# Second FFN: how many blocks' scatters wait for landings while the mixer runs

## The chip, the cores and the metric

One Trainium2 chip, one core of it, one launch. The metric is the device time of one execution in microseconds (us), the median of the runs. Engines are named as in the profile: PE (TensorE), DVE (VectorE), ACT (ScalarE), POOL (GpSimd), SP (SyncE, which here issues plain DMAs).

## The reference

Three layers on x of 4 sequences x 1,024 tokens x 128 features (4,096 tokens). The first and the third are the same mixture-of-experts FFN with the same weights:

```python
x = x + 0.5 * ffn(layernorm(x))        # 8 experts, top 2, and a shared one
x = x + attn(layernorm(x))             # mixer: conv, a recurrence over time, gated FFN
x = x + 0.5 * ffn(layernorm(x))

# ffn:
shared = (silu(x @ sw1) * (x @ sw2)) @ sw3
probs = softmax(x @ rw + rb); w, idx = top_k(probs, 2); w = w / sum(w)
gates = sum(w[..., None] * one_hot(idx, 8))
h = silu(x @ ew1[e]) * (x @ ew2[e]);  eout = h @ ew3[e]     # every expert e
out = shared + sum(eout * gates)
```

The middle layer keeps a state per head through a scan over the 1,024 tokens of each sequence; its own gated FFN has 352 hidden features.

## The kernel before

The 4,096 tokens are 8 blocks (NB) of 512, each 4 tiles (TT) of 128 rows. Blocks of the first FFN are turns 0 to 7, those of the second are turns 8 to 15. Both FFNs sort the rows by expert: each block is normalised (`dve_stats`, `pool_rstd`, `dve_norm` into `rows`), its logits and its rows' places are found (`dve_route`, `dve_places`, which ends with `pos_ready`), and POOL writes each row to two places of the DRAM tensor `xs`, with 8 indirect DMAs of 128 rows a block (`pool_scatter`, L710). All raise the semaphore `scattered` by 16 when they have landed. Then the shared expert is added, SP reads the 72 sorted tiles back from `xs` once `scattered` is at 1,024 per FFN and the last shared up-projection is done (L453 and the wait behind it), and the experts run over them; POOL scatters their answers to `ys` (L726), which SP reads back for the sum.

The second FFN's front is spread into the mixer. The mixer is a software pipeline: `in_order` calls one `body` per engine for steps n = -8 to 16, and `do(work, at(-k))` runs `work` for block n - k, if there is one. On POOL `route_rstd` is done for block n - 7 and `route_scatter` for block n - 9, in four pairs of scatters, of which the first stands ahead of `route_rstd`, the second behind it, the others behind `h_add`. `early` lets only blocks 0 to 4 (EARLY = 5) through; those of blocks 5 to 7 are issued behind the mixer by `pool_ffn(1)`, 24 in a row. So step 12 holds the scatters of block 3 and the rstd of block 5, step 13 the scatters of block 4 and the rstd of block 6, step 14 only the rstd of block 7, the last of all.

Each engine takes its instructions in program order; a wait on a semaphore holds what is behind it on that engine. Before each pair in the mixer POOL waits until every scatter before it has landed (L707 to L709). On DVE the norm of block 6 (turn 14, L1404) stands ahead of the mixer's last addition to x (L1324), and behind that come the statistics of block 7. The second FFN begins on PE (`pe_ffn_again`) when that last addition is done (`mixer_done`); the norm of block 7 stands behind the first two shared products on DVE (L1488), and the route of block 5 behind it; PE waits for what this route has chosen (`chosen`, L1989) ahead of the second block's second product.

Of the kernel before, what the change touches and what calls it, by code (L numbers as in the profile page):

```python
# [16 lines left out]
NB = TOK // BT  # L17
# [10 lines left out]
GROUP = 16  # L28

EARLY = 5  # L30
BACK = (4, NB)
LN_EPS = 1e-5

# [55 lines left out]
def macaron(nc, A, out):  # L89
    ctx = ExitStack()  # L90
    with ctx:
# [295 lines left out]
        def early(block):  # L387
            return block if block and SQ * block[0] + block[1] < EARLY else None

# [20 lines left out]
        def _(sp):  # L410
# [33 lines left out]
            for call in range(2):  # L444
# [18 lines left out]
                for r in range(YRING):  # L463
                    sp.wait_ge(y_stored[r], 32 * (NPAIR // YRING) * (call + 1))
                ring = BACK[call]
                for n in range(NB):
# [42 lines left out]
        def pool_mixer(pool, ffn_own):  # L509
# [134 lines left out]
            def route_scatter(b, q, k):  # L644

                pool_scatter(pool, NB + SQ * b + q, (2 * k, 2 * k + 1))
# [55 lines left out]
        def pool_scatter(pool, turn, which=range(2 * TT)):  # L702

            n = turn % NB
            pool.wait_ge(pos_ready, turn + 1)
            for i in which:
                if NB <= turn < NB + EARLY and i % 2 == 0:  # L707

                    pool.wait_ge(scattered, 16 * (turn * 2 * TT + i))  # L709
                pool.indirect_dma_start(xs, bass.IndirectOffsetOnAxis(pos[:, n, i:i + 1], 0),  # L710
                                        rows[:, n * TT + i % TT, :], None).then_inc(scattered, 16)
# [18 lines left out]
        def pool_ffn(pool, own, call):  # L730
            if call == 0:
                pool_rstd(pool, own, 0)
                pool_route_const(pool)
                pool_rstd(pool, own, 1)
                for n in range(NB):
                    pool_scatter(pool, n)
                    if n == 0:
                        pool_rstd(pool, own, 2, 2)
                    if n == 1:
                        pool_rstd(pool, own, 4, 4)  # L740
                pool_clear_features(pool)
                pool_mixer_const(pool)
            else:

                for n in range(EARLY, NB):
                    pool_scatter(pool, NB + n)
            for p in range(NPAIR):
                pool_answers(pool, call, p)
# [238 lines left out]
        def act_route_xt(act, n, answers):  # L987
            act.wait_ge(rx_ps_ready, n + 1)
            if n:

                act.wait_ge(logits_ps_ready, NB + n)
            act.activation(xr[:, :], answers, ACT.Copy).then_inc(rx_ready, 1)
# [8 lines left out]
        def act_silu(act, turn, k):  # L1001
            step = 2 * turn + k
            act.wait_ge(a_ps_ready, step + 1)
            if step >= 2:
                act.wait_ge(hid_done, step - 1)
            act.activation(silu_a[:, k, :], ps_a[:, k, :], ACT.Silu).then_inc(silu_done, 1)  # L1006
# [56 lines left out]
        def act_ffn_again(act):  # L1063
            act_xt(act, NB)
            act_xt(act, NB + 1)
            for n in range(NB):

                act_silu(act, NB + n, 0)
                if EARLY + n < NB:
                    act_route_xt(act, EARLY + n, ps_t)  # L1070
                act_silu(act, NB + n, 1)
# [365 lines left out]
        def dve_places(dve, own, turn, answers=ps_k):  # L1437

            n = turn % NB
            dve.wait_ge(rank_ps_ready, turn + 1)  # L1440
            own.step(dve.tensor_tensor(place[:, :].rearrange("p (t e) -> p t e", t=TT),
                                       answers[:, 0:TT * NE].rearrange("p (t e) -> p t e", t=TT),
                                       base[:, n:n + 1, :].broadcast_to([P, TT, NE]), ALU.add))
            dve.tensor_tensor(base[:, n + 1, :], base[:, n, :], answers[:, TT * NE:TT * NE + NE], ALU.add).then_inc(rank_read, 1)
            own.settle()
            own.step(dve.tensor_tensor(placed[:, :, :].rearrange("p (k t) e -> p k (t e)", k=2), hot[:, turn % 2, :, :],
                                       place[:, :].rearrange("p (a c) -> p a c", a=1).broadcast_to([P, 2, TT * NE]), ALU.mult))
            own.settle()
            own.step(dve.reduce_sum(pos_f[:, :], placed[:, :, :], axis=mybir.AxisListType.X))
            own.settle()  # L1450
            dve.tensor_copy(pos[:, n, :], pos_f[:, :]).then_inc(pos_ready, 1)
# [30 lines left out]
        def dve_hid(dve, turn, k):  # L1482
            step = 2 * turn + k
            dve.wait_ge(silu_done, step + 1)
            dve.wait_ge(b_ps_ready, step + 1)
            if turn >= 2:
                dve.wait_ge(down_ps_ready, turn - 1)
            dve.tensor_tensor(hid[:, turn % 2, k, :], silu_a[:, k, :], ps_b[:, k, :], ALU.mult).then_inc(hid_done, 1)  # L1488
# [44 lines left out]
        def dve_combine(dve, own, call, n):  # L1533

            dve.wait_ge(block_in[n], 16 * (call + 2))
            for k in range(2):
                for t in range(TT):
                    at = n * TT + t
                    r = dve.scalar_tensor_tensor(x[:, at, :], y_in[call][:, n % BACK[call], t, k * P:(k + 1) * P], share[:, k, at:at + 1],
                                                 x[:, at, :], ALU.mult, ALU.add)  # L1540
# [63 lines left out]
        def dve_ffn_again(dve, own):  # L1604
            dve.wait_ge(mixer_done, NB)
            for n in range(NB + 1):

                if n < NB:
                    dve_hid(dve, NB + n, 0)
                if 1 <= n <= NB - EARLY:  # L1610
                    dve_places(dve, own, NB + EARLY + n - 1)
# [596 lines left out]
```

## Time and profile before

| | |
|---|---|
| three runs | 786.61, 892.56 and 2213.87 us |
| median | 892.56 us |
| span of the profiled execution, first to last instruction | 783.3 us |
| its run time, taken as the shortest shown | 786.61 us, 3.3 us around the span |
| PE / DVE / ACT / POOL busy | 644.3 / 547.1 / 424.9 / 520.4 us |
| L710, scatters to xs | 128, 127.2 us busy, 993 ns each |
| L726, scatters to ys | 144, 141.0 us busy, 980 ns each |

"Busy" is the time in which an engine executes; POOL's row for a scatter is the time in which it makes and issues the transfer, not the transfer. Two parts of the profile say what that costs: the chain that ended last, which goes back from the last instruction to whatever released each one, and the timelines of the engines, where idle time ahead of an instruction stands in brackets with what ended it.

### The profile page before, as it was taken

How to read it: one execution, taken by the hardware profiler on the slowest of the kernel's cores; microseconds unless marked ns; L12 is line 12 of the kernel's file. 1: busy time of each engine (PE TensorE's matmuls, PEld its weight loads, DVE VectorE, ACT ScalarE, POOL GpSimd, SP SyncE). 2: the span in 40 equal slices, each digit the busy share in tenths (PEclk: the TensorE clock that was granted, in tenths of full speed). 3: DMA queues.
4: the chain of work that ended last, by engine and by line, in shares of the span. 5: the costliest groups of instructions: out<-in, count | busy, mean ns of one | idle time of the engine just before them, and what ended most of it. 6: DMA issues, size and time to landing. Idle time of an engine off the chain costs nothing.

```text
span 783.3 us, 13708 instructions
## 1 busy us (share of the span) xinstructions
PE 644.3 (82%) x3768; PEld 475.4 (61%) x3768; DVE 547.1 (70%) x1706; ACT 424.9 (54%) x745; POOL 520.4 (66%) x656
## 2 busy tenths in 40 slices
PE   3478979999916288989999998999968999999950
PEld 2245558888812045656575756577635667888840
DVE  4666756666539659897989999999743645666637
ACT  1122225455406999998999998764212324545525
POOL 3787775666645676896978869686765713666660
PEclk9989989999966678999999999999988999999995
DMA  9411223333242000000000000000000212333219
GB/s 266 159 46 52 82 67 80 93 89 85 65 142 84 0 1 1 0 2 1 1 2 1 2 15 15 14 15 15 28 27 28 69 45 76 87 89 91 81 30 318
DMA packets 49368, 46.34 MB, mean 59 GB/s; under 512 B 8456, under 2 KB 42861, under 8 KB 49296
## 3 DMA queue, kind: packets, MB, share of 16 engines
q1 hardware_dynamic: 40592, 28.54, 13.0%
q0 software_dynamic: 8704, 16.93, 6.7%
q8 instruction: 34, 0.56, 0.3%
q14 instruction: 38, 0.31, 0.1%
HBM read 25.30 MB, written 21.19 MB: 59 GB/s over the span
## 4 chain that ended last, share of the span: by engine, by line
PE 35%; POOL 24%; issue 15%; DVE 13%; ACT 8%; DMA 4%; POOLq 1%; SPq 0%; DVEq 0%; ACTq 0%
POOL ys L726 11%; POOL xs L710 10%; PE ps_tr L1662 4%; PE ps_go L1662 3%; DMA xs<-rows,pos 2%; PE ps_tr L2064 2%; PE ps_go L2012 2%; PE ps_go L2051 1%; PE ps_go L1833 1%; PE ps_tr L1850 1%; PE ps_go L1837 1%; POOL rstd L700 1%; PE ps_b L1884 1%; PE ps_a L2002 1%; PE ps_go L1883 1%
## 5 line engine op out<-in xcount | busy, mean ns | idle before, releaser
L726 POOL DMA_INDIRECT ys<-arena,dest x144 | 141.0, 980 | 99.8 <-issue 65.4
L710 POOL DMA_INDIRECT xs<-rows,pos x128 | 127.2, 993 | 58.8 <-issue 35.8
L1006 ACT ACTIVATE silu_a<-ps_a 128x512 f32<-128x512 f32 x32 | 19.1, 597 | 62.1 <-PE ps_a L2002 62.1
L2064 PE MATMUL ps_tr<-w_down_e,arena 128*128 x384 | 50.7, 275 | 0.0
L1521 DVE TENSOR_TENSOR hid<-silu_a,ps_a 128x512 f32<-128x512 f32 x36 | 24.8, 688 | 34.1 <-ACT silu_a L1026 34.1
L1521 DVE TENSOR_TENSOR hid<-silu_a,ps_b 128x512 f32<-128x512 f32 x36 | 24.8, 688 | 34.1 <-ACT silu_a L1026 34.1
L2064 PEld LDWEIGHTS ps_tr<-w_down_e,arena 128*128 128x128 f32 x384 | 46.7, 192 | 0.0
L1035 ACT ACTIVATE arena<-ps_go 128x512 f32<-128x512 f32 x72 | 42.6, 592 | 2.0 <-PE ps_go L2051 2.0
L1488 DVE TENSOR_TENSOR hid<-silu_a,ps_b 128x512 f32<-128x512 f32 x32 | 21.9, 686 | 31.0 <-PE ps_b L2004 29.1
L2051 PE MATMUL ps_go<-ident,hid 128*128 128x128 f32 x288 | 43.2, 273 | 0.2
L1026 ACT ACTIVATE silu_a<-ps_a 128x512 f32<-128x512 f32 x36 | 21.5, 597 | 38.1 <-PE ps_a L2040 38.1
L1026 ACT ACTIVATE silu_a<-ps_b 128x512 f32<-128x512 f32 x36 | 21.5, 597 | 37.7 <-PE ps_b L2040 37.7
L2051 PEld LDWEIGHTS ps_go<-ident,hid 128*128 128x128 f32 x288 | 35.5, 140 | 10.1 <-DVE hid L1521 0.8
L1018 ACT ACTIVATE xt_hi<-ps_tr 128x256 fp32r<-128x256 f32 x48 | 18.5, 385 | 35.0 <-PE ps_tr L2025 35.0
L1833 PE MATMUL ps_go<-arena,state 128*128 128x128 f32 x128 | 31.3, 329 | 7.4 <-DVE us L1291 6.5
L2012 PEld LDWEIGHTS ps_go<-w_shared_down,hid 128*128 128x128 f32 x256 | 31.6, 197 | 7.6 <-issue 7.6
L1963 PE MATMUL ps_tr<-ident,rows 128*128 128x128 f32 x64 | 13.5, 349 | 25.7 <-DVE rows L1404 19.9
L2012 PE MATMUL ps_go<-w_shared_down,hid 128*128 128x128 f32 x256 | 32.1, 280 | 1.7 <-DVE x L1493 1.7
L1833 PEld LDWEIGHTS ps_go<-arena,state 128*128 128x128 f32 x128 | 21.5, 201 | 19.4 <-issue 13.9
L2038 PE MATMUL ps_a<-up_hi,xt_hi 128*128 x72 | 31.8, 442 | 0.9 <-DVE xt_lo L1506 0.8
L1662 PE MATMUL ps_go<-arena,w_tap 128*128 128x512 f32 x64 | 32.2, 649 | 0.0
L2038 PE MATMUL ps_b<-up_hi,xt_hi 128*128 x72 | 31.6, 439 | 0.0
(368 smaller groups left out, 2032.5 us busy)
## 6 DMA issues: line engine op xcount, KB each, us to landing
arena<-xs SPq DMA_DIRECT2D x144, 65.0 KB, 1.9
rows<-ys SPq DMA_DIRECT2D x8, 512.0 KB, 3.7
arena<-ys SPq DMA_DIRECT2D x8, 512.0 KB, 6.8
ys<-arena,dest POOLq DMA_INDIRECT x144
x<-in_L_attn_x SPq DMA_DIRECT2D x8, 256.0 KB, 4.4
arena<-in_L_ffn_ew SPq DMA_DIRECT2D x4, 512.0 KB, 6.9
xs<-rows,pos POOLq DMA_INDIRECT x128
out<-x SPq DMA_DIRECT2D x8, 256.0 KB, 4.7
```

Source lines behind the costliest of these rows:

```text
L710: pool.indirect_dma_start(xs, bass.IndirectOffsetOnAxis(pos[:, n, i:i + 1], 0), rows[:, n * TT + i % TT, :], None).then_inc(scattered, 16)
L726: pool.indirect_dma_start(ys, bass.IndirectOffsetOnAxis(dest[:, i:i + 1], 0), y_out[:, p % YRING, j, :], None, bounds_check=2 * TOK - 1, o ...
L1026: act.activation(silu_a[:, p % 2, :].rearrange("p (j h) -> p j h", j=2), ps_pair[p % 2][:, :, 0:HID], ACT.Silu).then_inc(silu_e_done, 1)
L1035: act.activation(hid_t[:, p % 2, :], ps_d, ACT.Copy).then_inc(ht_ready, 1)
L1488: dve.tensor_tensor(hid[:, turn % 2, k, :], silu_a[:, k, :], ps_b[:, k, :], ALU.mult).then_inc(hid_done, 1)
L1521: dve.tensor_tensor(hid[:, p % 2, 0, :].rearrange("p (j h) -> p j h", j=2), silu_a[:, p % 2, :].rearrange("p (j h) -> p j h", j=2), ps_pai ...
L1662: r = pe.matmul(target, weights(k), zt[:, shift:shift + BT], start=(k == 0), stop=(k == taps - 1))
L1833: pe.matmul(pb["o"][:, at], state[:, k % 2, p * P:(p + 1) * P], cfs[:, q, k * P:(k + 1) * P], start=True, stop=False)
L2012: r = pe.matmul(ps_d[:, t * P:(t + 1) * P], hid[:, turn % 2, k, t * P:(t + 1) * P], w_shared_down[:, k, :], start=(k == 0), stop=(k == 1))
L2038: pe.matmul(target, xt_hi[:, p % 2, mine], hi, start=True, stop=False)
L2051: r = pe.transpose(ps_d[:, at:at + P], hid[:, p % 2, 0, at:at + P], ident[:, :])
L2064: r = pe.matmul(ps_answers(p)[:, j * P:(j + 1) * P], hid_t[:, p % 2, at:at + P], w_down_e[:, bass.ds(which[2 * p + j], 1), k, :].rearrange ...
```

## The change

One constant is added, and it takes the place of EARLY in the condition of the wait. EARLY, and so the place of every scatter, stays. The waits ahead of the pairs of turns 11 and 12 (blocks 3 and 4, 16 scatters, 8 waits) are gone; those of blocks 0 to 2 (12 waits) stay. No instruction is added, taken away or moved on any engine.

```diff
 EARLY = 5
+PACED = 3
 BACK = (4, NB)
 LN_EPS = 1e-5
...
             n = turn % NB
             pool.wait_ge(pos_ready, turn + 1)
             for i in which:
-                if NB <= turn < NB + EARLY and i % 2 == 0:
+                if NB <= turn < NB + PACED and i % 2 == 0:
 
                     pool.wait_ge(scattered, 16 * (turn * 2 * TT + i))
                 pool.indirect_dma_start(xs, bass.IndirectOffsetOnAxis(pos[:, n, i:i + 1], 0),
```

## Rows read from the trace of the kernel before

**Rows 1.** The page, part 4: the chain that ended last, by engine and line.
```profile
PE 35%; POOL 24%; issue 15%; DVE 13%; ACT 8%; DMA 4%; POOLq 1%; SPq 0%; DVEq 0%; ACTq 0%
POOL ys L726 11%; POOL xs L710 10%; PE ps_tr L1662 4%; PE ps_go L1662 3%; DMA xs<-rows,pos 2%; PE ps_tr L2064 2%; PE ps_go L2012 2%; PE ps_go L2051 1%; PE ps_go L1833 1%; PE ps_tr L1850 1%; PE ps_go L1837 1%; POOL rstd L700 1%; PE ps_b L1884 1%; PE ps_a L2002 1%; PE ps_go L1883 1%
```

**Rows 2.** Waits of POOL: who waited for what, us in total, times, longest us.
```profile
POOL xs L710 <- DMA xs<-rows,pos: 10.9, 5, 2.4
```

**Rows 3.** The chain in time, 545 to 650 us: start, length, what.
```profile
585.15 2.29 DMA xs<-rows,pos
...
595.17 1.05 POOL rstd L700
...
596.32 1.12 DVE rows L1404 x4
```

**Rows 4.** Timeline of POOL: start, length, instruction, [idle before <-releaser].
```profile
463.44 1.10 POOL L710 DMA_INDIRECT xs<-rows,pos  x1 [0.19 <-issue]
...
558.80 1.01 POOL L710 DMA_INDIRECT xs<-rows,pos  x1
...
563.17 1.10 POOL L710 DMA_INDIRECT xs<-rows,pos  x1 [0.68 <-issue]
...
575.11 0.96 POOL L710 DMA_INDIRECT xs<-rows,pos  x1 [2.10 <-DMA xs<-rows,pos]
...
579.43 0.96 POOL L710 DMA_INDIRECT xs<-rows,pos  x1 [2.09 <-DMA xs<-rows,pos]
...
582.03 1.04 POOL L700 TENSOR_TENSOR rstd<-var_eps,minus_half 128x4 f32<-128x4 f32 x1
583.76 1.09 POOL L710 DMA_INDIRECT xs<-rows,pos  x1 [0.68 <-issue]
...
588.21 0.96 POOL L710 DMA_INDIRECT xs<-rows,pos  x1 [2.09 <-DMA xs<-rows,pos]
...
592.58 0.96 POOL L710 DMA_INDIRECT xs<-rows,pos  x1 [2.15 <-DMA xs<-rows,pos]
...
602.50 0.96 POOL L710 DMA_INDIRECT xs<-rows,pos  x1 [0.30 <-issue]
...
630.33 0.96 POOL L710 DMA_INDIRECT xs<-rows,pos  x1 [0.30 <-issue]
```

**Rows 5.** L710 from 0 to 105 us: duration in ns, min/median/max.
```profile
L710 POOL DMA_INDIRECT xs<-rows,pos x64: 955/962/1307, 17.4 to 103.8; - x64
```

**Rows 6.** L710 from 430 to 600 us, the same columns.
```profile
L710 POOL DMA_INDIRECT xs<-rows,pos x40: 957/962/1447, 454.8 to 593.8; - x40
```

**Rows 7.** Timeline of DVE.
```profile
583.18 1.12 DVE L1404 TENSOR_SCALAR rows<-x,mv,rstd 128x128 f32<-128x128 f32 x4 [6.20 <-POOL rstd L700]
584.21 0.68 DVE L1324 TENSOR_TENSOR x<-x,ps_tr 128x512 f32<-128x512 f32 x1
...
585.84 0.38 DVE L1392 BATCH_NORM_AGGREGATE mv<-stats 128x2 f32<-128x6 f32 x4
...
592.90 0.69 DVE L1488 TENSOR_TENSOR hid<-silu_a,ps_b 128x512 f32<-128x512 f32 x1 [1.36 <-PE ps_b L2004]
```

**Rows 8.** Timeline of PE.
```profile
577.03 2.94 PE L1897 MATMUL ps_tr<-w_down,arena 128*128 128x128 f32 x24 [0.78 <-DVE arena L1318]
584.95 1.11 PE L1963 MATMUL ps_tr<-ident,rows 128*128 128x128 f32 x4 [4.97 <-DVE x L1324]
...
599.53 0.18 PE L1989 MATMUL ps_go<-chosen,earlier 128*128 128x32 bf16 x1 [3.28 <-DVE chosen L1434]
...
641.34 1.02 PE L2004 MATMUL ps_b<-arena,w_shared 128*128 128x512 f32 x2
```

**Rows 9.** Stretches: busy us of each engine, then PEclk (granted clock).
```profile
566.00:580.00 14.00, 12.21 (x72) 8.24 (x72) 7.57 (x39) 2.48 (x4) 8.92 (x11) 1.00 0.07 24
...
585.00:590.00 5.00, 4.22 (x11) 2.58 (x12) 1.18 (x8) 1.52 (x3) 2.45 (x3) 0.52 0.12 40
...
599.50:603.00 3.50, 3.47 (x13) 1.55 (x14) 1.25 (x6) 0.60 (x1) 1.59 (x2) 0.58 0.06 19
```

## The prediction

> **What bounds the kernel now.** I read first the chain that ended last. No engine holds it alone: PE has 35% of it, POOL 24%, and POOL's two kinds of scatter have 11% and 10% [rows 1]; the landings of scatters to xs are in it with 2%, some 16 us of 783.3. So a wait for a landing can be on the path. The waits of POOL say how much is plainly such: 10.9 us in five waits [rows 2]. The chain in order of time then shows where. At 585.15 us it goes through a landing of 2.29 us; it leaves POOL with the rstd of block 7 at 595.17 and goes on with DVE's norm of that block at 596.32 [rows 3]. The reader is to see that the end of the mixer hangs on POOL, and that POOL is slowed there by its own waits.
>
> POOL's timeline gives each wait its place [rows 4]. Of the five, the longest belongs to block 2 and stays. The other four lie in blocks 3 and 4: 2.10 at 575.11, 2.09 at 579.43, 2.09 at 588.21, 2.15 at 592.58. The first scatter behind each of the two rstds is late as well: 0.68 us of idle at 563.17 and at 583.76, against 0.19 behind an earlier one at 463.44, where the wait had long been met. The profile calls these "issue", but both come a landing's time behind the previous scatter.
>
> **What the change removes, step by step.** Of its eight waits two cost nothing now. The first of block 3 starts at 558.80 with no idle time ahead of it [rows 4]. The third pair of block 3 has POOL's h_norm and h_add between it and the pair before, which take longer than a landing. The cover stays, since nothing is moved; were it gone, each would cost the 1.8 us of its neighbours. The six others leave a gap of 0.30 us, as ahead of the unwaited scatter at 602.50 [rows 4], or of 0.19 behind an rstd:
>
> - 563.17: 0.68 - 0.19 = 0.49
> - 575.11: 2.10 - 0.30 = 1.80
> - 579.43: 2.09 - 0.30 = 1.79
> - 583.76: 0.68 - 0.19 = 0.49
> - 588.21: 2.09 - 0.30 = 1.79
> - 592.58: 2.15 - 0.30 = 1.85
>
> Sum 8.2 us for the rstd of block 7, and the first three, 4.1 us, for the rstd of block 6 (582.03, ends 583.07 [rows 4]).
>
> **Who takes it up.** DVE had waited 6.20 us for the rstd of block 6, with the mixer's last addition queued behind the norm (583.18, then 584.21); the statistics of block 7 end at 586.22, and PE had been idle 4.97 us for that addition [rows 7, 8]. PE's last mixer product, from 577.03, ends at 579.97 [rows 8], 0.5 sooner with POOL's first gain, and the addition would move to 580.1, so it is still DVE's queue that is late and all of the 4.1 us passes: the second FFN starts on PE at 580.9. The rstd of block 7 needs the statistics, now at 582.1, and POOL comes to it at about 587.0, so they don't hold it.
>
> Next, the norm of block 7 on DVE. It needs the rstd, which would end at 596.2 - 8.2 = 588.0, and DVE's second shared product, which ends at 593.59 - 4.1 = 589.5 [rows 7]. **What is late next** is thus that product: the norm moves from 596.32 to 589.6, by 6.8 us, and by the full 8.2 only if PE brings the product 1.4 us sooner.
>
> It may, by its clock. From 585 to 590 us the granted clock was 0.52, the lower level of 1.2 GHz, after the 4.97 us of idle; in 566 to 580, with pauses of about 1 us, it was 1.00, or 2.4 GHz [rows 8, 9]. The pause shrinks from 4.97 to about 1.4 us (579.5 to 580.9). If the clock stays up, 4.22 us of busy PE become 2.0 shorter at most (4.22 x 0.48), less what ACT's copies between them cover. Bounds 0 and 2.0 us, of which 1.4 count.
>
> The second pause, 3.28 us ahead of 599.53 for what the route of block 5 chose, shrinks to about 0.6 us (PE would be through at 596.2 - 4.1 = 592.1, the choice comes at 592.7), or to 1.2 in the other case. Behind it 3.5 us ran at 0.58 [rows 8, 9]; at 1.00 they take 1.5 us less. Bounds 0 and 1.5; I take 1.5, since pauses of that length left the clock at 1.00 in 566 to 580.
>
> The sum: 6.8 at least, 6.8 + 1.5 = 8.3 with the second clock term, 8.2 + 1.5 = 9.7 with both. Between the last two I take the middle, **9.0 us**.
>
> **What lies behind.** The 24 unwaited scatters of blocks 5 to 7 follow the route of block 5 and move with it; the last, at 630.33, is 11 us ahead of PE's last shared product at 641.34 [rows 4, 8], which also holds SP's reads of xs. So they bind neither before nor after. From there the experts' part has no tie to an earlier time: it shifts whole.
>
> **A page against it.** Scatters beside busy DVE took 957 to 1447 ns, median 962, and in the first FFN, with no waits, 955 to 1307 [rows 5, 6]. The Trainium skill, SBUF — State Buffer, in its section on SBUF's two separate sides, says that VectorE in a two-port mode locks GpSimd out of writing descriptors, so that a transfer issued by POOL can stand still for the length of a DVE instruction. By that rule the sum is the one of rival 1, not 9.0. This trace bears out little of it: the median is 5 ns off the minimum.
>
> **The time.** 783.3 - 9.0 = 774.3 us of span, with 3.3 us around it **777.6 us**. That stands on the shortest run shown, 786.61, to which the profiled execution belongs. The median, 892.56, is 106 us above, and the third run 1427 above; no row explains either. A like change on the level of the median would give 883.
>
> **The rivals.**
>
> 1. *Half of it is eaten* (0.12): unwaited scatters take longer beside DVE. If each of the 12 that follow 563 us took 0.49 us more, the worst seen over the median (1447 - 962), 5.8 of the 9.0 us would go: 783 us. It also stands for the norm of block 7 being held by something that I took to be covered. For: the 1447. Against: DVE is idle for much of 566 to 596, and 24 scatters in a row keep to 1.27 us.
> 2. *The excess of the longer runs sits in the waits* (0.15). If landings are what is slow there, 106 us over 20 waits is 5.3 each, and eight fewer give 42 more: 892.56 - 9 - 42 = 841. For: the only thing in this kernel that leaves the core unasked is DMA. Against: nothing shown of those runs.
> 3. *Slower* (0.13): with slow landings, unwaited scatters pile up, and each further one stalls in POOL's issue. In the longer runs the 88 + 144 unwaited transfers would carry the excess, 0.46 us each in the run of 892.56 and 6.2 in that of 2213.87; sixteen more add 7 or 98 us. It decides from (9.0 + 15.7) / 16 = 1.5 us per scatter on; below that it only eats the gain. A measured time in the 900s or above would be it. Against: in the profiled execution 88 run unwaited at 1.27 us apart.
> 4. *Nothing happens* (0.05): the waits were met by something else, such as the bare issue of POOL; then 786.6. The gaps of 0.30 beside those of 2.1 speak against it.
>
> The forecast itself has 0.55: of this some 0.12 is that the step holds and yet the number measured lies on the upper level, 875 to 895.
>
> **Range and chances.** The forecast's own range is 772 to 785: gain 6.8 to 9.7, and some us for how far the shortest run may lie from 786.6. With rivals 1, 2 and 4, and the upper level, the range goes from 770 to 895; rival 3 and the rest stay out. A difference of 2%, about 16 us, is what a measurement of this kernel can tell from no change. The forecast, 1.1%, is below it, and so are rivals 1 and 4: 0.60 for within 2%. Faster by more: rival 2, and the forecast if the two kernels' medians fall on different levels, 0.26. Slower by more: rival 3 and the same in reverse, 0.14.
>
> **What would show it.** In the profile after: no idle over 0.7 us ahead of any scatter from 558 us to the rstd of block 7, which starts near 587.0 and not 595.17; DVE's last addition near 580.1 and not 584.21; PE's pauses about 1.4 and 1 us in place of 4.97 and 3.28, with the granted clock near 1.00 behind both; and the rest as before, 9 us sooner. It is wrong if scatters there last over 1 us in the median, if the addition stays near 584 (another wait on DVE), or if the clock stays low behind the shorter pauses (then 6.8 us and 779.8).

## The result, and the profile after

| | before | after |
|---|---|---|
| runs | 785.39, 786.61, 892.56, 2213.87 us | 775.26, 777.01, 777.22, 778.66 us |
| median | 839.59 us | 777.12 us |
| profiled execution | span 783.3 | 775.26 us, span 773.5 |

Ratio 0.9893, 95% interval [0.9864, 0.9921]: 1.07% faster, 8.4 us of 786, and clear of no change. The ratio leaves out 892.56 and 2213.87, which have no like among the runs of the change. The profiled execution of the change is the fastest of its four (the spans of the others are 775.3, 775.5 and 776.9 us), so its trace shows somewhat more gain than the times do.

One figure ahead of the prediction is to be set right. The span of 783.3 us was taken to belong to the run of 786.61, with 3.3 us around it. In every later run the time is 1.7 to 2.2 us above the span, so it belongs to a run of about 785.3; the fourth run, 785.39, fits.

The page of the changed kernel, part 4, the chain that ended last:

```profile
PE 46%; POOL 18%; DVE 13%; issue 10%; ACT 8%; DMA 3%; SPq 1%; POOLq 0%; DVEq 0%; ACTq 0%
POOL xs L711 10%; POOL ys L727 5%; PE ps_tr L2065 4%; PE ps_tr L1663 4%; PE ps_go L2052 3%; PE ps_go L1663 3%; PE ps_go L2065 2%; PE ps_go L1834 2%; PE ps_a L2039 2%; PE ps_go L1838 2%; PE ps_a L2041 2%; PE ps_a L2040 2%; PE ps_go L2013 2%; PE ps_b L2041 2%; PE ps_b L2040 2%
```

POOL's share went from 24 to 18% and PE's from 35 to 46 [rows 1]. This doesn't measure the gain: the scatters to xs have 10% as before, and what fell, from 11 to 5%, is the share of the scatters to ys, which the change doesn't touch. The waits and the times do. POOL's waits for landings (us in total, times, longest us):

```profile
POOL xs L711 <- DMA xs<-rows,pos: 2.6, 1, 2.6
```

Five waits of 10.9 us have become one of 2.6, the one in block 2 that the change keeps [rows 2]. POOL's timeline (start us, length, instruction, idle before), then the durations of L711 (the old L710) from 555 to 600 us in ns, and the time from the issue of these scatters to their landing in us:

```profile
558.55 1.01 POOL L711 DMA_INDIRECT xs<-rows,pos  x1
...
562.44 1.10 POOL L711 DMA_INDIRECT xs<-rows,pos  x1 [0.20 <-issue]
...
572.41 0.95 POOL L711 DMA_INDIRECT xs<-rows,pos  x1 [0.30 <-issue]
...
574.93 0.96 POOL L711 DMA_INDIRECT xs<-rows,pos  x1 [0.30 <-issue]
...
577.54 1.04 POOL L701 TENSOR_TENSOR rstd<-var_eps,minus_half 128x4 f32<-128x4 f32 x1
578.78 1.09 POOL L711 DMA_INDIRECT xs<-rows,pos  x1 [0.20 <-issue]
...
581.44 0.96 POOL L711 DMA_INDIRECT xs<-rows,pos  x1 [0.30 <-issue]
...
583.96 0.95 POOL L711 DMA_INDIRECT xs<-rows,pos  x1 [0.30 <-issue]
...
586.55 1.04 POOL L701 TENSOR_TENSOR rstd<-var_eps,minus_half 128x4 f32<-128x4 f32 x1
...
621.67 0.95 POOL L711 DMA_INDIRECT xs<-rows,pos  x1 [0.30 <-issue]
```

```profile
L711 POOL DMA_INDIRECT xs<-rows,pos x23: 955/959/1098, 554.7 to 598.9; - x23
...
DMA to landing us min/median/max: 2.3/2.3/2.4
```

The six gaps of [rows 4] are now 0.20, 0.30, 0.30, 0.20, 0.30 and 0.30 us, and unwaited scatters take no longer: median 959 ns against 962 [rows 6], and none of them lands later than 2.4 us after its issue. The rstd of block 6 starts at 577.54 (was 582.03), that of block 7 at 586.55 (was 595.17). DVE's timeline:

```profile
578.69 1.21 DVE L1405 TENSOR_SCALAR rows<-x,mv,rstd 128x128 f32<-128x128 f32 x4 [2.21 <-POOL rstd L701]
579.73 0.68 DVE L1325 TENSOR_TENSOR x<-x,ps_tr 128x512 f32<-128x512 f32 x1
...
581.34 0.38 DVE L1393 BATCH_NORM_AGGREGATE mv<-stats 128x2 f32<-128x6 f32 x4
...
586.49 0.69 DVE L1489 TENSOR_TENSOR hid<-silu_a,ps_b 128x512 f32<-128x512 f32 x1 [1.36 <-PE ps_b L2005]
587.69 1.12 DVE L1405 TENSOR_SCALAR rows<-x,mv,rstd 128x128 f32<-128x128 f32 x4 [0.52 <-POOL rstd L701]
```

The last addition moved from 584.21 to 579.73, the norm of block 7 from 596.32 to 587.69 [rows 3, 7]. The norm still waits for the rstd (0.52 us), not for the shared product ahead of it, which ended at 587.18. PE's timeline, and the stretches (length, busy us of PE, PEld, DVE, ACT, POOL, then the granted clock):

```profile
576.53 2.94 PE L1898 MATMUL ps_tr<-w_down,arena 128*128 128x128 f32 x24 [0.78 <-DVE arena L1319]
580.46 0.66 PE L1964 MATMUL ps_tr<-ident,rows 128*128 128x128 f32 x4 [0.98 <-DVE x L1325]
...
590.91 0.18 PE L1990 MATMUL ps_go<-chosen,earlier 128*128 128x32 bf16 x1 [1.08 <-DVE chosen L1435]
...
631.43 1.02 PE L2005 MATMUL ps_b<-arena,w_shared 128*128 128x512 f32 x2
```

```profile
585.00:590.00 5.00, 4.83 (x24) 2.87 (x22) 3.06 (x20) 2.23 (x5) 2.25 (x3) 1.00 0.08 28
590.00:596.00 6.00, 5.09 (x40) 4.17 (x41) 2.75 (x12) 1.66 (x3) 2.90 (x3) 1.00 0.08 25
```

The pauses of 4.97 and 3.28 us have shrunk to 0.98 and 1.08, and the granted clock, 0.52 and 0.58 behind them before, is 1.00 throughout [rows 8, 9]. The last shared product ends 9.9 us sooner, the last scatter (621.67) is still 10 us ahead of it, and the span is 9.8 us shorter. To see what the clock's part is, take the way from PE's L1989 (599.53 before, 590.91 after) to the first scatter of an answer, which stands in POOL's timelines, of before and of after:

```profile
657.26 0.99 POOL L726 DMA_INDIRECT ys<-arena,dest  x1 [25.98 <-DVE arena L1531]
```

```profile
647.34 1.00 POOL L727 DMA_INDIRECT ys<-arena,dest  x1 [24.71 <-DVE arena L1532]
```

57.73 us before, 56.43 after: 1.3 us less. With the 8.6 by which L1989 came sooner that is 9.9, all of the 9.8. That the 1.3 is the clock's is borne out by the traces further down, under "The clock alone".

### The profile page after: what moved, and what is told of

It reads as the page before. It is cut to its first block, busy times and chain, and to the rows that moved or that the text cites. A ratio compares the mean times of both kernels' runs of the same rounds, so it can differ in the third digit from the quotient of the medians.

```text
span 773.5 us, 13700 instructions
## 1 busy us (share of the span) xinstructions
PE 641.4 (83%) x3768; PEld 473.3 (61%) x3768; DVE 546.6 (71%) x1706; ACT 424.6 (55%) x745; POOL 519.9 (67%) x656
## 4 chain that ended last, share of the span: by engine, by line
PE 46%; POOL 18%; DVE 13%; issue 10%; ACT 8%; DMA 3%; SPq 1%; POOLq 0%; DVEq 0%; ACTq 0%
POOL xs L711 10%; POOL ys L727 5%; PE ps_tr L2065 4%; PE ps_tr L1663 4%; PE ps_go L2052 3%; PE ps_go L1663 3%; PE ps_go L2065 2%; PE ps_go L1834 2%; PE ps_a L2039 2%; PE ps_go L1838 2%; PE ps_a L2041 2%; PE ps_a L2040 2%; PE ps_go L2013 2%; PE ps_b L2041 2%; PE ps_b L2040 2%
## 5 line engine op out<-in xcount | busy, mean ns | idle before, releaser
L711 POOL DMA_INDIRECT xs<-rows,pos x128 | 127.2, 993 | 50.8 <-issue 36.0
L1838 PE MATMUL ps_go<-gram,tm 128*64 128x128 f32 x256 | 30.7, 321 | 0.0
```

What stands on the lines that cost most here:

```text
L1838: r = pe.matmul(pb["o"][i * DH:(i + 1) * DH, at], tm[:, k % 2, h * DH:(h + 1) * DH], gram[:, k % 2, :, h, :], start=False, stop=True)
```

## The experiments

Ratios are to runs of the kernel before on the same chip. The level differs between chips: on two the kernel before takes 785 us, on three others 850. Each was used in one session, so a chip and a session can't be told apart. A number is compared only within one chip.

**What a comparison can tell.** The constant at 5 makes a copy.

```diff
-PACED = 3
+PACED = 5
```

> The changed source with the constant at 5, so every wait is as before: a copy of the kernel before. It measures what the comparison itself can tell. Theory: ratio 1.000, interval within 0.4% either way, so a gain of 1.1% is well clear. Rival: the copies differ by 1% or more, and then the measured 1.1% could be chance. It also shows how often a run of the waits-everywhere kernel is far above 786 us; the theory has no opinion on that.

On a chip at 851 us: 0.9948 [0.9910, 0.9986]; the copy is off by 0.5%. Again:

> The copy of the kernel before, on a chip where it takes about 785 us. Theory: ratio 1.000 with an interval of 0.3% or less either way, so that 1.07% is clear of it. Rival: it is off by 0.5% as on the chip at 850 us, and half of the measured gain could be that.

It fell on a chip at 853 us: 1.0019 [0.9987, 1.0051]. So there 0.5% is not to be trusted and 1% is about the limit. The question for 785 us was not answered by a copy; the nearest thing is the variant with products in the pauses, further down, at 1.0005 [0.9981, 1.0028].

The copy also tells of the long level. POOL's waits for landings in it, and ACT's two largest waits:

```profile
POOL xs L711 <- DMA xs<-rows,pos: 12.9, 7, 2.6
```

```profile
ACT silu_a L1007 <- remote: 50.5, 7, 16.6
ACT xt_hi L1019 <- remote: 46.2, 18, 3.3
```

POOL's waits for landings are 12.9 us in 7 waits, against 10.9 in 5 at 785 us, so no more than 2 of the 65 us are theirs. ACT meanwhile waits nearly 100 us for something that the profile calls "remote" and doesn't know, on a kernel with one core. The chain that ended last has it too:

```profile
PE 41%; DVE 15%; issue 14%; another core or an unknown queue 10%; ACT 10%; POOL 6%; DMA 4%; SPq 0%; POOLq 0%; DVEq 0%; ACTq 0%
```

10% of 850.9 us is 85 us, as large as the excess. All ten traces from the chips at 850 us have such lines, and none of the ten at 785 has one. The scatters themselves are no slower: the median is 959 ns to xs and 981 to ys, against 962 and 982 before. What the unknown releaser is stays open.

**Block 4 alone.**

```diff
-PACED = 3
+PACED = 4
```

> Waits dropped for block 4 alone (4 waits, 79.43 us range after 579). Theory: the rstd of block 6 comes 1.8 us sooner, the rstd of block 7 5.9 us sooner; the norm of block 7 is then held by DVE's second shared product at 591.8 (4.5 us) or, if the clock stays up behind the first pause (about 3.2 us), by the rstd (5.9); 1.5 us more from the clock behind the second pause. Sum 6.0 to 7.4 us, ratio 0.991 to 0.992. Rival (only the sum of waits counts, no clock): 4.5 to 5.9.

At 851 us: 0.9879 [0.9830, 0.9929]. The repeat at 785 us:

> Block 4's waits dropped alone, once more, on a chip where the kernel before takes about 785 us. Theory as before (waits plus clock): 6.0 to 7.4 us. Rival (waits alone): 4.5 to 5.9.

0.9918 [0.9894, 0.9942], 6.4 us of 784.9. DVE's norm of block 7, and two stretches:

```profile
593.21 1.11 DVE L1405 TENSOR_SCALAR rows<-x,mv,rstd 128x128 f32<-128x128 f32 x4
```

```profile
585.00:590.00 5.00, 4.33 (x9) 2.19 (x10) 0.04 (x1) 1.72 (x3) 3.98 (x6) 0.50 0.16 53
...
599.50:603.00 3.50, 3.50 (x24) 2.70 (x23) 1.25 (x8) 1.05 (x2) 2.76 (x3) 1.00 0.18 57
```

The norm starts with no idle ahead of it: the shared product holds it, since the clock behind the first pause is still low (0.50). The second stretch is at 1.00. That is the case "held by the second shared product, clock back behind the second pause" of the expectation. Its size is not met in the trace: the norm came at 593.21 in place of 591.8, so 3.1 us sooner and not 4.5, and the span is 4.5 us shorter and not 6.0. The profiled run is the slowest of the six. The times, 6.4 us with an interval of 4.6 to 8.3, hold 6.0 and most of the rival's 4.5 to 5.9 as well; it is the trace that speaks for the clock.

**Block 3 alone.**

```diff
-                if NB <= turn < NB + EARLY and i % 2 == 0:
+                if NB <= turn < NB + EARLY and turn != NB + 3 and i % 2 == 0:
```

> Waits dropped for block 3 alone (4 waits). Theory: both rstds come 2.3 us sooner (0.49 + 1.80), the second pause of PE stays above 3 us and its clock low, so the run gains 2.3 us, ratio 0.997. Rival (the clock returns with either pause): 3.8 us. Rival (block 3's waits are covered): 0.

At 851 us: 0.9885 [0.9810, 0.9959], nearly as much as the whole change; with a copy off by 0.5% on that chip I don't read it. At 785 us:

> Block 3's waits dropped alone, once more, on such a chip. Theory: 2.3 us. Rival (clock comes back too): 3.8 or more; rival (covered): 0.

0.9974 [0.9957, 0.9991], 2.0 us. PE's timeline and two stretches behind:

```profile
597.45 0.18 PE L1989 MATMUL ps_go<-chosen,earlier 128*128 128x32 bf16 x1 [3.04 <-DVE chosen L1434]
```

```profile
599.50:603.00 3.50, 3.50 (x16) 2.98 (x15) 0.69 (x1) 0.14 (x1) 2.59 (x4) 0.50 0.12 38
603.00:605.50 2.50, 2.50 (x14) 2.50 (x13) 0.00 (x0) 0.46 (x1) 1.89 (x3) 0.50 0.17 53
```

The second pause is still 3.04 us and the clock behind it 0.50, as expected. The interval of the times, 0.7 to 3.4 us, leaves out both rivals (0 and 3.8). 2.0 and 6.4 add up to the 8.4 of the change, though with intervals this wide the exact fit is chance. The trace also shows what nobody expected: the clock came back only at about 605.6 us, 8 us behind the pause, where the kernel before had it back about 4 us behind a pause of 3.28. This profiled run, 785.5 us, is the slowest of twelve, and its span of 783.4 us shows none of the gain.

**No waits at all in the mixer.**

```diff
-PACED = 3
+PACED = 0
```

> No waits for landings in the mixer at all. Theory: blocks 0 to 2 have one wait that shows (2.44 us of idle at 553.17), and behind it POOL waits for DVE's us anyway (0.56 at 557.38), so at most 0.5 us beyond the measured change: ratio 0.988 to 0.990. Rival (waits in the middle of the mixer protect something): slower than the change, scatters over 1 us in the median, or some runs far above 780.

> No waits in the mixer, once more, on such a chip. Theory: no more than 0.5 us beyond the change, 774.5 to 777 us. Rival (the waits of blocks 0 to 2 protect something): slower than the change.

> No waits in the mixer, beside the changed kernel on one chip. Theory: within 0.5 us of the changed kernel. Rival: 1 to 2 us below it, if the wait of 2.44 us in block 2 was on the path.

0.9889 [0.9836, 0.9941] at 851 us, 0.9877 [0.9846, 0.9909] at 785, 0.9922 [0.9890, 0.9953] at 853, where the changed kernel itself, run beside it,

> The changed kernel again. Theory: 8.4 to 9.7 us, ratio 0.9877 to 0.9893. Rival: nearer to the sum of the waits' direct effect on the start alone (4.1 us, 0.995).

had 0.9914 [0.9882, 0.9945]. The waits of blocks 0 to 2 cost nothing that can be measured, nor do they protect anything that shows. The trace at 785 us (the slowest of its four runs) bears on the prediction in another way. PE's start, and a stretch behind it:

```profile
582.67 0.66 PE L1964 MATMUL ps_tr<-ident,rows 128*128 128x128 f32 x4 [1.39 <-DVE x L1325]
```

```profile
584.00:587.00 3.00, 2.90 (x7) 1.90 (x8) 0.00 (x0) 0.66 (x2) 2.39 (x3) 0.50 0.16 53
```

The pause is 1.39 us, just the length that was predicted for the change, and the clock behind it is 0.50. The shared product was late by it, and the norm of block 7 started behind that product, at 590.79.

**Which rstd counts.** All waits kept; the rstd of block 6 goes ahead of block 4's first pair. Two small helpers choose the block: but_last passes every block but 4, only_last passes 4 alone.

```diff
-                do(route_scatter, early(at(-9)), 0)
+                do(route_scatter, but_last(early(at(-9))), 0)
                 do(route_rstd, at(-7))
+                do(route_scatter, only_last(at(-9)), 0)
```

> All waits kept; in step 13 the rstd of block 6 stands ahead of block 4's first pair. Theory: that rstd ends near 578.7 in place of 583.07, so the second FFN starts on PE 4.2 us sooner, but the rstd of block 7 stays at 595.2 behind the same waits, and PE then waits longer in the second pause (about 8 us): gain 0 to 0.5 us. Rival (the start of the second FFN sets the end): 4.2 us, ratio 0.9947.

1.0060 [1.0035, 1.0086]: 4.7 us slower, which neither expected. POOL's timeline, PE's, and two stretches:

```profile
577.00 1.04 POOL L707 TENSOR_TENSOR rstd<-var_eps,minus_half 128x4 f32<-128x4 f32 x1
...
589.35 0.96 POOL L717 DMA_INDIRECT xs<-rows,pos  x1 [3.60 <-DMA xs<-rows,pos]
...
596.32 1.04 POOL L707 TENSOR_TENSOR rstd<-var_eps,minus_half 128x4 f32<-128x4 f32 x1
```

```profile
580.04 0.66 PE L1970 MATMUL ps_tr<-ident,rows 128*128 128x128 f32 x4 [0.78 <-DVE x L1331]
...
600.68 0.18 PE L1996 MATMUL ps_go<-chosen,earlier 128*128 128x32 bf16 x1 [11.26 <-DVE chosen L1441]
```

```profile
600.00:603.00 3.00, 2.32 (x11) 1.32 (x12) 1.84 (x9) 0.02 (x1) 0.73 (x1) 0.50 0.00 0
...
606.00:609.00 3.00, 3.00 (x15) 3.00 (x16) 0.00 (x0) 0.60 (x1) 2.20 (x3) 0.50 0.16 50
```

The start came at 580.04, nearly 5 us sooner, as expected. The rstd of block 7 didn't, and PE stood idle for 11.26 us. I had priced a longer pause at nothing. Behind it the clock was at the lower level until about 609 us, over 8 us; in the kernel before it is back after about 4. A landing was slow too (3.60 us of wait at 589.35), and the rstd starts at 596.32, 1.2 later than before. From L1996 to the first answer's scatter it is 60.60 us against 57.73. The 2.9 and the 1.2 are nearly all of the 4.2 us by which the span is longer. So the rstd of block 7 sets the end, and a start that runs ahead of it gains nothing. That it loses is shown by the times; that the longer pause is what held the clock down is not, since block 3 alone had 8 us at the lower level behind a pause of 3.04.

**The same waits elsewhere.** Block 4's last two pairs go behind the rstd of block 7.

```diff
                 do(route_rstd, at(-7))
+                do(route_scatter, only_last(at(-10)), 2)
+                do(route_scatter, only_last(at(-10)), 3)
...
-                do(route_scatter, early(at(-9)), 2)
+                do(route_scatter, but_last(early(at(-9))), 2)
...
-                do(route_scatter, early(at(-9)), 3)
+                do(route_scatter, but_last(early(at(-9))), 3)
```

> All waits kept; block 4's last two pairs stand behind the rstd of block 7 in place of ahead of it. Theory: that rstd comes as soon as its statistics, about 586.3 us, the norm is then held by DVE's second product (593.6, 2.7 us sooner), and the clock returns behind the shortened second pause (1.5 us): 4.2 us, ratio 0.9947, with the two pairs' waits moved to where PE covers them. Rival (what the waits cost is lost wherever they stand): 0.

0.9966 [0.9947, 0.9986], 2.7 us (1.1 to 4.2), with every wait still there. POOL's timeline and DVE's:

```profile
586.69 1.04 POOL L708 TENSOR_TENSOR rstd<-var_eps,minus_half 128x4 f32<-128x4 f32 x1
```

```profile
594.06 0.69 DVE L1496 TENSOR_TENSOR hid<-silu_a,ps_b 128x512 f32<-128x512 f32 x1 [1.77 <-PE ps_b L2012]
594.67 1.11 DVE L1412 TENSOR_SCALAR rows<-x,mv,rstd 128x128 f32<-128x128 f32 x4
```

The rstd comes at 586.69 as expected, and the norm is held by the shared product; but that came at 594.06 and not at 592.90, because the clock behind the first pause stayed low for longer this time: it is 0.50 from 590 to 592 us, and was 1.00 there before, though the pause is 5.04 us against 4.97. That is the missing 1.2 us. It is where the waits stand that makes them dear.

**The clock alone.** PE gets products that nobody reads, in both pauses; no wait of POOL is touched.

```diff
-            pe.wait_ge(mixer_done, NB)
             pe.wait_ge(rank_read, NB + EARLY)
+            for _ in range(5):
+                pe.matmul(ps_k[:, :], w_shared[:, 0:P], w_shared[:, 0:BT], start=True, stop=True)
+            pe.wait_ge(mixer_done, NB)
...
                     pe.wait_ge(rank_read, NB + late - 1)
+                    if n == 1:
+                        for _ in range(3):
+                            pe.matmul(ps_k[:, :], w_shared[:, 0:P], w_shared[:, 0:BT], start=True, stop=True)
                     pe_rank(pe, NB + late - 1)
```

> The kernel before with PE kept busy in its two pauses by products that nobody reads: five of 128x512 while it waits for the mixer's last addition, three before it waits for what block 5's route chose. No wait of POOL is changed. Theory: granted clock 1.00 from 585 to 603 us; the first pause gives nothing (the rstd of block 7 binds), the second 1.5 us: ratio 0.998. Rival (the clock has no part, only the waits): 0, or slower by the products. Rival (both stretches pay): 2.5 to 3.5 us.

1.0005 [0.9981, 1.0028]. PE's timeline and two stretches:

```profile
579.29 4.46 PE L2102 MATMUL ps_go<-w_shared 128*128 128x512 f32 x10
...
593.63 2.74 PE L2120 MATMUL ps_go<-w_shared 128*128 128x512 f32 x6
599.52 0.21 PE L1989 MATMUL ps_go<-chosen,earlier 128*128 128x32 bf16 x1 [3.15 <-DVE chosen L1434]
```

```profile
585.00:590.00 5.00, 4.22 (x17) 2.41 (x17) 1.33 (x7) 2.86 (x5) 2.55 (x3) 1.00 0.14 43
...
599.50:603.00 3.50, 3.48 (x12) 1.73 (x13) 1.32 (x6) 0.60 (x1) 1.52 (x2) 0.53 0.06 19
```

The first pause was filled and the clock behind it 1.00: no gain, since the rstd of block 7 binds. But PE came to the second pause sooner, the three products were done at 596.4, it stood idle for 3.15 us and fell to 0.53 again. So the second half of the test had failed. With six products there:

> As the kernel with products in PE's two pauses, but six in the second, so that it is busy until about 598.8 us. (With three, it stood idle for 3.15 us all the same and ran at the lower level behind that.) Theory: granted clock near 1.00 from 599.5 to 603 and a gain of 1.5 us, the waits untouched. Rival (the clock has no part in the gain): 0.

```profile
592.96 5.32 PE L2120 MATMUL ps_go<-w_shared 128*128 128x512 f32 x12
598.60 0.19 PE L1989 MATMUL ps_go<-chosen,earlier 128*128 128x32 bf16 x1 [0.33 <-DVE chosen L1434]
```

```profile
599.50:603.00 3.50, 3.50 (x25) 2.78 (x25) 1.09 (x4) 1.19 (x2) 2.13 (x3) 1.00 0.06 19
```

```profile
654.73 0.99 POOL L726 DMA_INDIRECT ys<-arena,dest  x1 [23.92 <-DVE arena L1531]
```

The pause is 0.33 us, the clock 1.00, and from L1989 to the first answer's scatter it is 56.13 us, 1.6 less than the 57.73 of before. The whole run gives 0.9993 [0.9975, 1.0012], 0.5 us, an interval from 2.0 us faster to 0.9 slower. The trace shows the term, the times don't resolve it.

The same way, in the nine traces at 785 us that keep the first FFN as it was, goes by the clock. Where it was 1.00 behind the second pause it takes 56.09 us (block 4 alone), 56.09 (no waits), 56.13 (this kernel), 56.25 (the waits moved) and 56.43 (the change). Where it fell it takes 57.73 (before), 57.77 (three products), 59.74 (block 3 alone) and 60.60 (the rstd of block 6 first).

**Waits everywhere.**

```diff
-                if NB <= turn < NB + EARLY and i % 2 == 0:
+                if turn + i > 0 and i % 2 == 0:
```

> A wait for landings ahead of every second scatter to xs, those of the first FFN and the last 24 of the second too (64 in all). Theory: each pair takes 4.3 us in place of 2.5; 32 pairs on the chain of the first FFN cost up to 57 us, the last 12 cost 22 less the 11 of slack, so 840 to 855 us. Rival for the long runs seen of the kernel before (they come with waits for landings): with three times the waits, most runs are far above the fastest. Without that tie the share of long runs is as before.

1.0736 [1.0699, 1.0773], 843.1 us median, within the 840 to 855 worked out; the five runs lie within 2 us of each other. The profile shows 92.3 us in 46 waits for landings, 81.4 more than before, of which 58 reached the time. They brought none of the five runs far above the others.

**The two together.** No waits, and both moves.

> No waits in the mixer; in step 13 the rstd of block 6 stands ahead of block 4's first pair, and block 4's last two pairs stand behind the rstd of block 7. Theory: PE's last mixer product (579.5) and DVE's second shared product bind now; the start gains 0.2 us and the norm of block 7 0.7, so 0.7 to 1.2 us below the changed kernel, ratio 0.987 to 0.988. Rival: the later scatters hold something, and it is as the changed kernel or slower.

> The reordered version without waits once more. Theory: 0.7 to 1.2 us below the changed kernel on a chip at 785 us. Rival: the same as the changed kernel.

> The changed kernel once more, beside e_best's kernel. Theory: ratio 0.988 to 0.990 on a chip at 785 us, 0.991 on one at 850.

At 853 us it had 0.9932 [0.9900, 0.9963], beside the changed kernel's 0.9914; at 850 us 0.9860 [0.9820, 0.9901], beside 0.9875 [0.9832, 0.9918]. Neither tells it from the changed kernel, and it never ran on a chip at 785 us.

## Why the prediction was right, and where it was not

- **The six gaps.** Predicted 8.2 us for the rstd of block 7, 4.1 for that of block 6. In the profile 8.62 and 4.49, of which the gaps are 8.2 and 4.1; 0.25 of each is older (558.55 against 558.80), 0.19 is a shorter L611 (1.04 us against 1.23). Shown.
- **Who takes it up.** The addition was predicted at 580.1, it came at 579.73. The norm of block 7 was to be held by the shared product at 589.6, or with the clock by the rstd at 588.1; it was the rstd, 587.69. With block 4 alone the product did hold it. Both branches have thus been seen.
- **The clock.** Predicted 1.00 behind pauses of about 1.4 and 1 us; so it was, behind 0.98 and 1.08. The term of 1.5 us measured 1.3 here and 1.6 in the variant with filled pauses. That the first pause left the clock up was in part luck: behind 1.39 us, in the kernel without waits, it fell to 0.50. What decides is not shown; the middle of the two branches, which the prediction took, says no more than that.
- **The sum.** 9.0 us predicted, 9.8 in the profiled execution (the fastest of four), 8.4 [6.2, 10.7] in the times; 777.6 against 777.12. That these last two are so close is luck in part: 3.3 us around the span was some 1.3 too much, and the 9.0 some 0.6 more than the times show. The times don't tell the branches of 8.3 and 9.7 apart.
- **The rival of DVE eating half** is out: the median of the unwaited scatters is 959 ns. The Trainium skill's rule on the shared port (SBUF — State Buffer, the section on its two separate sides) would have brought it about; in this stretch the longest scatter takes 1,098 ns on POOL, 0.14 us above the median, and the longest landing 2.4 us against a median of 2.3, so nothing here is held up for the length of a DVE instruction; in which mode DVE ran, no row shows. The single long one, 1,447 ns before, stands ahead of this stretch.
- **The step that failed is "range and chances".** "A difference of 2%, about 16 us, is what a measurement of this kernel can tell from no change": no row stood behind it, and it is not so. The change came out at 0.9893 [0.9864, 0.9921], and at 785 us the intervals of the other comparisons are 0.2 to 0.3% wide either way, so 1.1% is clear of no change. The measured difference does lie within 2%, and as a statement on its size the 0.60 held; as a forecast that nothing could be told, it was put on the wrong outcome. My own argument had only two cases with a gain well under 9 us, of 0.12 and 0.05. "Faster by about 1%, and told" was what the sum of the gaps said.
- **The base was left open too.** Against the median shown, 892.56, the forecast of 777.6 would be 13% faster; against the shortest run it is 1.1%. The sum was built on the shortest, and the runs bear that out: 1.07% against runs of 785 to 787 us. The level of 892.56 was never met again.
- **The upper end of 895** took in 892.56 as a level that the change could land on. The levels found are 785 and 850 us, and they go with the chip, as far as one session on each can tell: 50 runs of the kernel before lay between 782.8 and 791.2 on two chips, 59 between 842.8 and 860.6 on three. None came near 892.56 or 2213.87, and those two stay unexplained.
- **Rivals 2 and 3** tied the excess to landings or to unwaited scatters. With waits everywhere nothing strays in five runs, and with none in the mixer nothing does in 22; at 850 us POOL's waits for landings carry at most 2 of 65 us, and its scatters are as short as at 785. Both are out for the 850 level; for the two lone runs they could not be tried.

## What to carry to other kernels

A wait for a transfer costs what it delays, so find the instruction behind it on its queue that others wait for: here all of POOL's 8.2 us passed, because two small rstd instructions stood behind the scatters, and moving the scatters behind the rstd gave 2.7 us with the waits still in place. Price a pause of PE by its length and by what the clock does behind it; a start made sooner that only lengthens a later pause can lose. And ask of a measurement what a comparison on one chip resolves before calling a predicted gain small.

## What the runs showed of the hardware that was not expected

- The length of PE's pause doesn't tell how long the lower clock (0.50) lasts behind it. Read from stretches of 2 us, it was back at 1.00 about 4 us after a pause of 3.28 (before), 8 after one of 3.04 (block 3 alone), 5 and 7 after 4.97 and 5.04 (before, and the waits moved), and 9 after 11.26 (the rstd of block 6 first). Behind one of 1.39 us it fell as well (no waits), while one of 1.34 at 566 us in the kernel before and those of 0.33 to 1.08 us left it at 1.00.
- The variant with the pause of 11.26 us took 4.7 us more, though its work had started 5 us sooner.
- The same kernel takes 785 us on two chips and 850 on three others, one session on each. Only the traces at 850 us have waits whose releaser the profile can't name (in the copy 10% of the chain), on engines that had been waiting for each other.
